# Splitting two pieces of an expert's hidden layer in one VectorE operation

## What is computed

```
logits = xf @ gate_w
probs = jax.nn.softmax(logits, axis=-1)
dispatch_w, expert_idx = jax.lax.top_k(probs, TOP_K)
combine = jnp.sum(jax.nn.one_hot(expert_idx, E, dtype=xf.dtype) * dispatch_w[..., None], axis=1)
for e in range(E):
    h = jax.nn.gelu(xf @ w1[e] + b1[e], approximate=False)
    y = h @ w2[e] + b2[e]
    out = out + combine[:, e:e + 1] * y
return x + out.reshape(B, S, D)
```

## Time and profile before

| | us |
|---|---|
| median of 3 runs | 1255.43 |
| lowest and highest | 1252.72, 1256.72 |
| the profiled execution | 1255.06 |
| its span | 1253.2 |
| TensorE, VectorE, ScalarE busy | 1154.5, 822.1, 545.5 |
| VectorE: casts of h, subtractions of h | 91.0, 123.0 |

### The profile page before, as it was taken

The page is one execution under the profiler, slowest core; times in us unless marked ns, Lnnn a source line. Parts: engine busy times, 40 slices in busy tenths (PEclk is TensorE's granted clock), DMA queues, the critical chain, the costliest instruction groups (busy, mean ns, idle before and its releaser), DMA issues.

```text
span 1253.2 us, 25051 instructions
## 1 busy us (share of the span) xinstructions
PE 1154.5 (92%) x8118; PEld 1075.5 (86%) x8119; DVE 822.1 (66%) x1883; ACT 545.5 (44%) x995; POOL 342.7 (27%) x352
## 2 busy tenths in 40 slices
PE   6999999999999999999999335999999999999993
PEld 5897998988988889989888234899999999999992
DVE  4675475954667744768436777796797678856651
ACT  2533445432435334454334313674574556644431
POOL 0010002500004300025000325355455455555440
PEclk9999999999999999999999658899999999999996
DMA  5000000200001100011000133363563547533238
GB/s 164 1 4 31 1 1 1 69 34 1 1 2 35 68 1 1 1 35 35 1 1 1 62 112 106 104 198 53 170 201 52 155 90 216 147 59 54 55 46 273
DMA packets 66207, 82.70 MB, mean 66 GB/s; under 512 B 11105, under 2 KB 56545, under 8 KB 66145
## 3 DMA queue, kind: packets, MB, share of 16 engines
q1 hardware_dynamic: 52128, 63.48, 15.6%
q0 software_dynamic: 14016, 18.37, 8.2%
HBM read 60.85 MB, written 22.02 MB: 66 GB/s over the span
## 4 chain that ended last, share of the span: by engine, by line
PE 81%; DVE 8%; DMA 4%; issue 3%; SPq 1%; ACT 1%; DVEq 1%; POOL 0%; ACTq 0%; POOLq 0%
PE ps L1545 74%; PE ps L1625 2%; DMA w1r<-in_w 2%; PE ps L1587 1%; PE ps L1835 1%; PE ps L1558 1%; DMA rows<-acc_rows 1%; DVE w2s L1466 1%; DVE hs L1512 1%; DVE one_hot L1095 1%; DVE pick_hi L1103 1%; PE ps L1578 1%; PE ps L1634 1%; PE ps L1647 1%; DVE pick_lo L1098 1%
## 5 line engine op out<-in xcount | busy, mean ns | idle before, releaser
L1545 PE MATMUL ps<-xt,w1s 128*128 128x256 f32 x1746 | 257.8, 284 | 1.5 <-DVE xt L1476 1.5
L1545 PE MATMUL ps<-w2s,hs 128*128 128x256 f32 x1728 | 251.1, 280 | 2.8 <-DVE hs L1514 2.7
L1545 PEld LDWEIGHTS ps<-xt,w1s 128*128 128x128 f32 x1746 | 227.7, 190 | 2.1 <-DVE xt L1476 1.9
L1545 PEld LDWEIGHTS ps<-w2s,hs 128*128 128x128 f32 x1728 | 223.6, 188 | 4.2 <-issue 4.1
L944 ACT ACTIVATE h<-ps,b1t 128x256 f32<-128x256 f32 x288 | 137.3, 477 | 114.0 <-PE ps L1545 79.0
L704 POOL DMA_INDIRECT acc_rows<-y_w,now_s x72 | 119.8, 1665 | 166.2 <-issue 155.1
L1512 DVE CAST hs<-h 128x256 fp32r<-128x256 f32 x288 | 91.0, 316 | 71.0 <-ACT h L944 35.9
L1514 DVE TENSOR_TENSOR hs<-h,hs 128x256 fp32r<-128x256 f32 x288 | 123.0, 427 | 9.9
L1545 PE MATMUL ps<-xs,wh 128*128 128x512 f32 x384 | 123.1, 401 | 1.5 <-issue 1.5
L586 POOL TENSOR_TENSOR tl_r<-tl_eps,minus_half 128x4 f32<-128x4 f32 x16 | 16.2, 1014 | 350.8 <-DVE tl_eps L1216 350.8
L691 POOL DMA_INDIRECT xg<-xf_rows,now_g x76 | 93.2, 1226 | 47.3 <-POOL now_g L687 34.7
(11 more groups left out here) (213 smaller groups left out, 1871.5 us busy)
## 6 DMA issues: line engine op xcount, KB each, us to landing
w1r<-in_w SPq DMA_DIRECT2D x16, 1024.0 KB, 5.1
w2r<-in_w SPq DMA_DIRECT2D x16, 1024.0 KB, 8.9
b2t<-in_b SPq DMA_DIRECT2D x36, 128.0 KB, 2.9
xn<-in_x SPq DMA_DIRECT2D x4, 1024.0 KB, 4.9
acc_rows<-r_out SPq DMA_DIRECT2D x4, 1024.0 KB, 4.5
xf_rows<-xf SPq DMA_DIRECT2D x4, 1024.0 KB, 4.9
rows<-acc_rows SPq DMA_DIRECT2D x8, 512.0 KB, 7.4
out_tokens<-cols_out SPq DMA_DIRECT2D x8, 512.0 KB, 9.0
```

The lines of the kernel that those rows point to most:

```text
L1545: ins = t.matmul(out, left[l], right[r], start=first and n == 0, stop=last and n == 2, **more)
```

## The change

Two neighbouring pieces, f and f + 1, are split together: at even f VectorE waits for both gelus and for both old second products, does one CAST and one subtraction of 128x512, and counts h_hi and h_lo up by two. At odd f it splits nothing. The other work of the loop (y_bias, x_lo, the weight pieces) keeps its place by f. No other engine's program changes.

```
                 for f in range(FC):
                     gi = n * FC + f
-                    dve.wait_ge(h_act, at(i, 2 * FC, gi + 1))
-                    if not (first and n == 0):
-                        dve.wait_ge(y_mm, at(i, 2 * FC, gi + 1 - FC))
-                    v.tensor_copy(hs[0][:, f, :], h32[:, gi % 4, :]).then_inc(h_hi, 1)
-                    dve.wait_ge(h_hi, at(i, 2 * FC, gi + 1))
-                    v.tensor_tensor(hs[1][:, f, :], h32[:, gi % 4, :], hs[0][:, f, :].bitcast(F32),
-                                    ALU.subtract).then_inc(h_lo, 1)
+                    if f % 2 == 0:
+                        dve.wait_ge(h_act, at(i, 2 * FC, gi + 2))
+                        if not (first and n == 0):
+                            dve.wait_ge(y_mm, at(i, 2 * FC, gi + 2 - FC))
+                        c = slice(gi % 4, gi % 4 + 2)
+                        v.tensor_copy(hs[0][:, f:f + 2, :], h32[:, c, :]).then_inc(h_hi, 2)
+                        dve.wait_ge(h_hi, at(i, 2 * FC, gi + 2))
+                        v.tensor_tensor(hs[1][:, f:f + 2, :], h32[:, c, :], hs[0][:, f:f + 2, :].bitcast(F32),
+                                        ALU.subtract).then_inc(h_lo, 2)
                     if f == 1 and not (first and n == 0):
```

## The result

The changed kernel takes **1277.41 us** (median of 4 runs, 1274.53 to 1281.21), the kernel before beside it 1254.08 (1251.05 to 1256.72). The ratio is 1.0182, with a 95% interval of 1.0145 to 1.0219: 23 us slower. The prediction was 1278, within 1268 to 1289. The profiled execution took 1274.53, its span is 1272.0.

The account below looks back on a forecast made before the run. TensorE was taken to bound the kernel (busy 92% of the span, without a gap in the stretch read). Terms 22.0 + 3.5 + 1.2 + 1.2 - 5.0 = +22.9 on 1255 gave 1278, range 1268 to 1289.

Parts of the forecast that it names:

- chain through X: Transposes, eviction, gelu of piece 3, joined split, second product of piece 2: 0.61 late in each of 36 steps, +22.0.
- turns, and load of w1r: First second product late by 0.5 at seven loop turns, +3.5; 0.15 at eight weight steps where ScalarE awaits w1r, +1.2.
- start: First step of the expert stage: the first second product must also wait for the gelu of piece 1, +1.2 once.
- today's waits: The 5.0 the expert stage loses to TensorE's waits at seven loop turns in the kernel before, credited as -5.0.
- Part 1: VectorE's work: larger casts and subtractions cut its busy time by 53, worth nothing by itself behind TensorE.
- Parts 2 and 3: Joined split's latency, and its wait for piece 3's gelu behind the transposes: 0.61 lost per step, +22.0.
- latency of 1.36: From the start of a joined cast to the waiting second product: 0.42 + 0.03 + 0.69 + 0.22.
- Part 4: The other pairs, second products of pieces 4, 6 and next step's 0: slack 0.6 to 0.7, so no cost.
- rival C: More pairs late: one more place in each step waits 0.25, 9 more, 1287; chance 0.12.
- Part 5: Seven loop turns after weight steps: late by 0.5 each, +3.5; load of w1r at eight others, +1.2.
- A: Rival: the latency behind the transposes is hidden because recorded end times overlap; about 1256, no change; chance 0.11.
- B: Rival: VectorE's reduced work removes all seven waits and the pairs are always in time; 1251, faster; chance 0.05.

Follow-up runs that it names:

- (2,3) alone: Kernel before, with only pieces 2 and 3 split together and the other six one by one: 1276.97 us, ratio 1.0180.
- the late eviction: ScalarE's eviction of the transposed rows moved behind the gelu of piece 3: changed kernel 1260.17 us, ratio 1.0052; kernel before 1254.61, ratio 1.0001.
- (4,5) alone: Kernel before, with only pieces 4 and 5 split together and the other six one by one: 1259.58 us, ratio 1.0066.
- (0,1) alone: Kernel before, with only pieces 0 and 1 split together and the other six one by one: 1261.93 us, ratio 1.0085.
- experiment 3: Kernel before, no pairs, sixth weight piece moved behind piece 7's split: 1255.1 us, ratio 1.0014; compared with only pieces 6 and 7 joined, 1248.47.
- pair (6,7): Kernel before, with only pieces 6 and 7 split together and the other six one by one: 1248.47 us, ratio 0.9944.

## Why the prediction was right, point by point

The total held, 23.3 against 22.9, and that it is so close is partly luck: the chain was put 2.9 too low, the turns and the load 2.1 too high. The terms, with what the traces show:

| term | forecast | measured | from |
|---|---|---|---|
| chain through X | 22.0 | 24.9 | 35 x 0.69 = 24.2; last X to TensorE's last block 11.18, was 10.47 |
| turns, and load of w1r | 3.5 + 1.2 | 2.6 | 437.86 - 35 x 12.437 |
| start | 1.2 | 1.1 | first F to first X 6.58, was 5.51 |
| today's waits | -5.0 | -5.0 | |
| sum | 22.9 | 23.6 | |

The two profiled executions differ by less, 19.5, since in that of after the stage began 3.3 earlier; nothing in the change reaches that far, and the medians differ by 23.3.

- **Part 1.** Right that VectorE's saving is not on the path. The two groups lost 27.4 and 23.2, 51 in place of 53; the engine only 41. That fits recorded operations that overlap the next one (868.42 + 0.69 = 869.11, the next starts at 869.03), with half as many ends to overlap.
- **Parts 2 and 3.** The mechanism is shown by the chain of waits, by (2,3) alone and by the late eviction. The step that was mis-sized is the latency of 1.36 and what stands ahead of it. G(3)'s end to S(2) was forecast at 0.13 + 1.36 = 1.49 and takes 869.24 - 867.70 = 1.54: 0.19 + 0.43 + 0.10 + 0.69 + 0.13. The count by two adds 0.14, and the gap from subtraction to matmul is 0.13, not the 0.22 that I had read at S(0) and used for S(2). The block after the wait takes 0.83, not 0.81. The rest of the 0.08 is rounding in rows of two digits. The trace of before has both operations at this size in the attention stage, which I used for their durations only:

```profile
94.77 0.42 DVE L1333 CAST us<-prob 128x512 fp32r<-128x512 f32 x1
95.22 0.69 DVE L1335 TENSOR_TENSOR us<-prob,us 128x512 fp32r<-128x512 f32 x1
```

  They count by one and their gap is 0.03, as forecast. That the new operations count by two stands in the diff, but no engine's operation in the kernel before counts so, and no row priced it.
- **Part 4.** The other pairs do fit in the changed kernel, but not by slacks of their own, as I had it. I worked them out in a step without weight pieces. In a weight step (4,5) is late, and (0,1) at the turn behind it or at the load, which (4,5) alone and (0,1) alone show; in the changed kernel the wait at S(2) hides most of it. So the mechanism of rival C exists, in weight steps and not in each step, and waits behind the forecast's own.
- **Part 5.** The term that failed is the 0.5 at each of the seven turns. It took the 0.97 that the kernel before shows behind two pieces and put it whole behind three. In after, VectorE and then TensorE there:

```profile
836.01 0.69 DVE L1516 TENSOR_TENSOR hs<-h,hs 128x512 fp32r<-128x512 f32 x1
836.62 1.89 DVE L1466 TENSOR_TENSOR w2s<-w2r,w2s 128x512 fp32r<-128x512 f32 x3
838.81 0.43 DVE L1514 CAST hs<-h 128x512 fp32r<-128x512 f32 x1 [0.29 <-ACT h L944]
...
840.28 0.96 PE L1547 MATMUL ps<-w2s,hs 128*128 128x256 f32 x6
```

  Pieces 5 to 7 run without a gap, the cast follows 0.30 after them, not 0.97, and S(0) has no wait. From the start of the pair's subtraction to the next cast the forecast had 10.73 - 7.28 = 3.45, and it takes 838.81 - 836.01 = 2.80; experiment 3 shows where the difference goes. With two pieces last the term is real: (2,3) alone loses 0.5 to 0.6 at each of five turns. The load of w1r bit once, at 825.15 (a wait of 1.80 on ScalarE), with 0.79 at S(0) and a period of 13.44.
- **Rivals.** A and B are out: the gap between end and matmul is real time (0.13 at every S(2)), and relief comes only with pair (6,7), whose two inputs have slack.

Of the Trainium skill's two sentences (Perfetto Trace Analysis, Optimizing Scalar/DVE Operations) the one on bubbles agrees with the traces: (2,3) joined gives 36 waits, and breaking the subtraction up again took 0.34 off each step. The one on grouping asks for a saturated engine. VectorE was busy 66% of the span, so it did not promise a gain, and none came from all four pairs; (6,7) removed 4.8 us at turns where VectorE was what came last.

## What to carry to other kernels

A joined operation starts with its latest input and releases its first output with its last: list for each joined pair what its second input waits for in the queue of the engine that makes it (here an eviction that waited for TensorE's transposes, a weight cast that waited for a load) and what stands ahead of the joined operation in its own engine's queue (here the loop turn), in the busiest kind of step, not the plainest. Join only where both ends have slack; here one pair in four did, and that one gave 0.56% where all four cost 1.8%. When a change makes one engine late by the same amount in every step, its other costs may be hidden behind that, so taking the main cause away returns less than it seemed to cost.

## What the runs showed of the hardware

- An operation that counts a semaphore up by two starts 0.07 later behind what releases it than the same operation counting by one: 0.19 against 0.12 for the cast, 0.10 against 0.03 for the subtraction; 12.44, 12.37 and 12.30 a step with two, one and none of them.
- Behind VectorE's last subtraction before a loop turn the next cast starts 2.60 after that subtraction's start with two weight pieces between (836.88 to 839.48), 2.73 with three (832.59 to 835.32): 0.60 more work, 0.13 more time. The idle gap that a turn shows depends on how much work is queued ahead of it.
- Casts of 128x512 have a median of 0.427 but reach 0.632 in the changed kernel. None in the chain through X of the steps read was stretched.
- From a subtraction's end to the matmul that waits for it: 0.13 at S(2) (869.11 to 869.24) and S(4) (910.80 to 910.93), 0.25 at S(0) in the run of (0,1) alone (827.03 to 827.28). Why S(0) takes longer was not tried.
